# Second attention layer: one score unit as two halves of two heads, and its logarithm one place later

## The reference

```python
def _stablemax3_s(x):
    pos = 1.0 + x * (1.0 + 0.5 * x * (1.0 + x / 3.0))
    neg = 1.0 / (1.0 - x * (1.0 - 0.5 * x * (1.0 - x / 3.0)))
    return jnp.where(x >= 0, pos, neg)

def stablemax3(logits, axis=-1):
    logits = logits - jnp.max(logits, axis=axis, keepdims=True)
    s = _stablemax3_s(logits)
    return s / jnp.sum(s, axis=axis, keepdims=True)
...
attn = jnp.einsum('bhsd,bhtd->bhst', q, k) * scale
attn = stablemax3(attn, axis=-1)
out = jnp.einsum('bhst,bhtd->bhsd', attn, v)
```

## Time and profile before

| what | value |
|---|---|
| median of 3 runs | 5062.23 us (5046.65 to 5062.62) |
| the profiled execution | 5072.4 us, around a span of 5070.6 us |
| mean granted clock of PE over the span | 0.856 |
| PE, DVE, ACT, POOL busy | 3905.7, 2461.1, 1575.5, 323.2 us |
| from the first to the last square of the stage | 541.8 us |
| its busy time: PE, DVE, ACT | 404.8, 228.6, 449.5 us of 545.3 |

### The profile page before, as it was taken

The page is one execution under the profiler, slowest core; times in us unless marked ns, Lnnn a source line. Parts: engine busy times, 40 slices in busy tenths (PEclk is TensorE's granted clock), DMA queues, the critical chain, the costliest instruction groups (busy, mean ns, idle before and its releaser), DMA issues. The chain is left out here.

```text
span 5070.6 us, 97683 instructions
## 1 busy us (share of the span) xinstructions
PE 3905.7 (77%) x38224; PEld 2797.4 (55%) x38224; DVE 2461.1 (49%) x6959; ACT 1575.5 (31%) x2611; POOL 323.2 (6%) x451
## 2 busy tenths in 40 slices
PE   1259737988796999946887777568888888888899
PEld 1236524656465777733443333257667676676776
DVE  8636544532241000024554444277667676676762
ACT  0012202235202222211217888223322323323331
POOL 0011110000032000041000000000000000000000
PEclk8579868999757999977987787579999999999997
DMA  1281131011224454432000000200000000000000
GB/s 32 80 352 32 41 124 53 19 27 31 67 94 173 175 175 175 173 123 77 16 14 15 13 17 13 103 6 12 9 11 8 9 12 9 11 8 9 8 6 3
DMA packets 162722, 296.02 MB, mean 58 GB/s; under 512 B 36688, under 2 KB 138944, under 8 KB 154480
## 3 DMA queue, kind: packets, MB, share of 16 engines
q1 hardware_dynamic: 118336, 195.52, 12.5%
q10 hardware_dynamic: 37680, 77.59, 4.0%
q0 software_dynamic: 6272, 16.85, 1.0%
HBM read 184.17 MB, written 105.20 MB: 57 GB/s over the span
## 5 line engine op out<-in xcount | busy, mean ns | idle before, releaser
L2242 PE MATMUL peer_total<-peer_up,peer_hid 128*128 128x256 f32 (+1 forms) x2112 | 603.5, 410 | 2.2
L2172 PE MATMUL peer_work<-peer_xnT,peer_down 128*128 128x256 f32 (+1 forms) x2176 | 564.0, 388 | 41.0 <-issue 40.3
L2172 PEld LDWEIGHTS peer_work<-peer_xnT,peer_down 128*128 128x128 f32 x2176 | 428.6, 203 | 130.1 <-issue 50.5
L2269 ACT ACTIVATE peer_hid<-peer_work 128x256 f32<-128x256 f32 (+1 forms) x544 | 202.0, 371 | 833.5 <-PE peer_work L2172 833.5
L2230 PE MATMUL peer_scat<-peer_one_j,peer_one_i 64*64 64x32 f32 x16448 | 319.9, 228 | 136.7 <-DVE peer_one_j L2373 106.6
L2242 PEld LDWEIGHTS peer_total<-peer_up,peer_hid 128*128 128x128 f32 (+1 forms) x2112 | 379.7, 192 | 71.4 <-issue 10.8
L2230 PEld LDWEIGHTS peer_scat<-peer_one_j,peer_one_i 64*64 64x64 f32 x16448 | 293.0, 144 | 223.3 <-issue 223.2
L2291 ACT ACTIVATE peer_G<-peer_scat 128x512 f32<-128x512 f32 x258 | 273.0, 1058 | 360.0 <-PE peer_scat L2230 360.0
L2390 DVE TENSOR_TENSOR peer_hid<-peer_hid,peer_G 128x256 f32<-128x256 f32 (+1 forms) x544 | 215.6, 408 | 321.3 <-ACT peer_hid L2269 304.4
L1723 PE MATMUL moe_bank<-moe_xgT,moe_w 128*128 128x256 f32 x1280 | 294.9, 384 | 52.9 <-ACT moe_mid L1802 45.6
L1945 DVE TENSOR_TENSOR moe_yb<-moe_bank,moe_w 128x512 f32<-128x512 f32 x40 | 27.7, 692 | 624.5 <-PE moe_bank L1735 624.5
(11 more groups left out here) (361 smaller groups left out, 6250.5 us busy)
## 6 DMA issues: line engine op xcount, KB each, us to landing
moe_w<-in_moe_w SPq DMA_DIRECT2D x40, 2180.0 KB, 8.8
ys<-ret_zeros ACTq DMA_DIRECT2D x16, 2296.0 KB, 52.5
moe_xg<-xs SPq DMA_DIRECT2D x40, 256.0 KB, 8.8
ys<-moe_yb ACTq DMA_DIRECT2D x40, 256.0 KB, 9.1
soft_xT<-xT SPq DMA_DIRECT2D x32, 257.0 KB, 2.8
stable_xT<-xT SPq DMA_DIRECT2D x32, 257.0 KB, 2.8
ret_xT<-xT SPq DMA_DIRECT2D x16, 257.0 KB, 2.8
aT<-ret_cN SPq DMA_DIRECT2D x64, 64.2 KB, 2.1
```

The source lines that it names most:

```text
L2172: last = mm(work[:, jj % 2, 0:nb], down[:, c, jj, :], xnT[:, q, c, 0:nb], start=c == 0, stop=c == DC - 1)
L2242: last = mm(total[:b_rows, j, :], hid[:, e % NHID, j * P:j * P + b_rows], up[:, e, :], start=e == 0 and j == 0, stop=e == JB - 1, skip_gro ...
L2269: A(hid[:, jj % NHID, 0:nb], work[:, jj % 2, 0:nb], ACT.Gelu).then_inc(gelu_ready, 1)
```

## The change

A unit's four banks are treated as two halves of two banks (two heads). PE makes the scores of the first two heads as soon as DVE has freed their banks, tells ACT, waits for the other two banks and makes the other two. ACT squares each half by an instruction of its own, DVE multiplies and adds each half by an instruction of its own and frees the half's banks. The logarithm and the exponential still take a whole unit, but the logarithm of a unit now stands behind the first half-square of the next unit, and the exponential behind its second half-square. The first attention layer keeps its order.

```diff
@@ scores (PE)
-                else:
+                elif causal:
                     pe.wait_ge(s_taken, n)
...
                 stand()
+                if not causal:
+                    for x in range(2):
+                        if n:
+                            pe.wait_ge(s_taken, 2 * n + x - 1)
+                            stand()
+                        for j in range(2 * x, 2 * x + 2):
+                            rows = slice(SLOT * j, SLOT * j + SLOT)
+                            last = mm(S[:, j, 0:T], KT[rows, g, hg, k * P:k * P + P], QT[rows, g, hg, :], start=True, stop=True)
+                        last.then_inc(s_ready, 1)
+                    return
...
@@ weigh, log (ACT)
-                else:
-                    if n >= 2:
-                        act.wait_ge(ln_ready, n - 1)
-                    A(U[:, n % 2, :, :], S[:, :, 0:T], ACT.Square, scale=-SCALE, bias=bend[:, :]).then_inc(y_ready, 1)
-
-            def log(g, v):
-                n = g * SU + v
-                act.wait_ge(t_ready, n + 1)
...
+            def square(n, x):
+                act.wait_ge(s_ready, 2 * n + x + 1)
+                if n >= 2:
+                    act.wait_ge(ln_ready, n - 1)
+                A(U[:, n % 2, 2 * x:2 * x + 2, :], S[:, 2 * x:2 * x + 2, 0:T], ACT.Square, scale=-SCALE, bias=bend[:, :])\
+                    .then_inc(y_ready, 1)
+
+            def log(n):
+                act.wait_ge(t_ready, 2 * n + 2)
                 if n >= nw:
                     act.wait_ge(av_done, (n - nw) // 2 + 1)
                 A(W[:, n % nw, :, :], U[:, n % 2, :, :], ACT.Ln, scale=-1.0).then_inc(ln_ready, 1)
@@ the order on ACT
-                        weigh(g, v)
-                        if not causal and g + v:
-                            exponential(g * SU + v - 1)
-                        if not causal:
-                            log(g, v)
+                        if causal:
+                            weigh(g, v)
+                        else:
+                            n = g * SU + v
+                            square(n, 0)
+                            if n:
+                                log(n - 1)
+                            square(n, 1)
+                            if n:
+                                exponential(n - 1)
                     if not causal and g == B and s == 0:
+                        log(B * SU - 1)
                         exponential(B * SU - 1)
@@ cubic (DVE)
-                u = U[:, n % 2, :, :]
-                dve.wait_ge(y_ready, n + 1)
-                v_.scalar_tensor_tensor(u, u, REST, S[:, :, 0:T], ALU.add, ALU.mult).then_inc(t_ready, 1)
-                dve.wait_ge(t_ready, n + 1)
-                dve.sem_inc(s_taken, 1)
+                for x in range(2):
+                    u = U[:, n % 2, 2 * x:2 * x + 2, :]
+                    dve.wait_ge(y_ready, 2 * n + x + 1)
+                    v_.scalar_tensor_tensor(u, u, REST, S[:, 2 * x:2 * x + 2, 0:T], ALU.add, ALU.mult).then_inc(t_ready, 1)
+                    dve.wait_ge(t_ready, 2 * n + x + 1)
+                    dve.sem_inc(s_taken, 1)
```

More of the change, by code:

```diff
@@ L1050, in scores @@
                 stand()
+                if not causal:
[8 more added lines that the diff above has]
+                    return
                 for j in range(SLOTS):
                     rows = slice(SLOT * j, SLOT * j + SLOT)
-                    if causal:
-                        mm(S[:, j, 0:T], KT[rows, g, hg, 0:P], QT[rows, g, hg, :], start=True, stop=False, skip_group_check=True)
-                    else:
[L1056 to L1063, removed]
+                    mm(S[:, j, 0:T], KT[rows, g, hg, 0:P], QT[rows, g, hg, :], start=True, stop=False, skip_group_check=True)
+                for j in range(SLOTS):
+                    rows = slice(SLOT * j, SLOT * j + SLOT)
+                    mm(S[:, j, T:SPAN], KT[rows, g, hg, P:2 * P], QT[rows, g, hg, P:T], start=False, stop=False, skip_group_check=True)
+                for j in range(SLOTS):
+                    for at in (0, T):
+                        last = masked(S[:, j, :], at, 1)
                 last.then_inc(s_ready, 1)
@@ L1183, in weigh @@
                 act.wait_ge(s_ready, n + 1)
[L1184 to L1190, removed]
-                    if n >= 2:
-                        act.wait_ge(ln_ready, n - 1)
-                    A(U[:, n % 2, :, :], S[:, :, 0:T], ACT.Square, scale=-SCALE, bias=bend[:, :]).then_inc(y_ready, 1)
-            def log(g, v):
-                n = g * SU + v
-                act.wait_ge(t_ready, n + 1)
+                if n >= nw:
+                    act.wait_ge(av_done, n - nw + 1)
+                A(W[:, n % nw, :, :], S[:, :, 0:SPAN], ACT.Exp, scale=SCALE).then_inc(w_ready, 1)
+                act.wait_ge(w_ready, n + 1)
+                act.sem_inc(s_taken, 1)
+            def square(n, x):
[6 more added lines that the diff above has]
+                act.wait_ge(t_ready, 2 * n + 2)
                 if n >= nw:
```

## The result

The changed kernel takes 5100.5 us (median of 5 runs, 5095.7 to 5115.5) where the kernel before takes 5059.6 (5 runs): a ratio of 1.0093, 95% interval 1.0071 to 1.0115. It is slower by about 41 us, well clear of that interval.

What follows compares the result with a forecast made beforehand. The prediction took the ring and PE's clock to bound the stage. A batch falls from 34.1 to 31.6 us, times 16 a gain of 40, so the median goes from 5062.2 to 5022 us; range 4990 to 5060.

Steps and rivals of the forecast that it cites:

- second rival: In the stage, even units' scores queue behind earlier products at half clock: kernel slower, 5096 us at clock 0.77; chance 0.09.
- the same line: Forecast time of a batch after the change against PE's granted clock c: 30.0 + 27.0 (1 - c) us.
- ACT and DVE: ACT's unit 3.07 us, half-squares 0.67, logarithm's wait from 50 to under 10 us; DVE's half multiply-adds 0.73, covered.
- PE at full clock: A pair of scores keeps PE as long as four; lateness adds 0.9, so a batch takes 30.0 us against 31.5.
- PE at half clock: Doubled scores make PE the bound: a pair of units takes 8.8 us against 7.96, 3.4 more a batch.
- The clock: PE's usual granted clock in the stage taken as 0.91, with PE held 82% at full clock; a batch 31.6 us.
- become shorter: Argument against the no-change rival (chance 0.13): PE's idle stretches, 2.01 us before scores, shrink.
- packing: Four heads' scores run side by side on PE; splitting into pairs adds 83 us of PE time; no-change chance 0.13.
- a clock at or below 0.85 with ACT waiting for scores after products: Sign of being wrong: low granted clock in the stage while ACT waits for scores queued behind PE's products.
- DVE's copies delaying the first multiply-add: Sign of being wrong: on DVE, copies hold up a unit's first half multiply-add; no size given.
- break-even clock: Granted clock of 0.85 in the stage, under which the forecast batch exceeds the 34.1 us of before.
- the ring: In a unit before the change: square, multiply-add, logarithm, then ACT free for the next square, 3.36 us.

Runs made afterwards that it cites:

- e4: The changed kernel plus five discarded matmuls a batch where PE stood idle, behind the spreads of units 4 and 6: 5017.2 us, 0.9920 of before.
- e13: The changed kernel plus five discarded matmuls a batch behind the products of unit 7, where PE leaves no gap: 5142.7 us, 1.0171 of before.
- e7: The changed kernel plus three discarded matmuls a batch, behind the spread of unit 6 only: 5059.4 us, 1.0001 of before.
- e1: The kernel before with only the logarithm moved behind the next unit's square, nothing halved: 5019.2 us, 0.9918 of before.
- e2: The changed kernel with ACT's old order: half-squares side by side, exponential of the unit before, then this unit's logarithm: 5054.1 us, 0.9996 of before.
- e3: Halves on ACT and DVE in the old order, but PE's four heads of scores made side by side: 5016.2 us, 0.9918 of before.
- e14: Whole scores, halves on ACT and DVE, logarithm behind both half-squares, first value unit two steps later, no added matmuls: 5038.1 us, 0.9956 of before.
- e10: The changed kernel with the first value unit at step 3 instead of 1: 5099.4 us, 1.0073 of before.

## Why the prediction was wrong

The forecast was 5022 us, a gain of 40; the kernel lost 41. The mechanism was in the main the one that the prediction had as its second rival, "PE becomes the bound at half clock", at a chance of 0.09: ACT waits 57.0 us for scores queued behind other work of PE. What the rival did not name is the odd score at half clock, 47.5 us of ACT's waits. That its 5096 us lies near the measured 5100 is luck: it belongs to a clock of 0.77, and at the measured 0.68 the same line gives 38.6 us a batch, 72 us more than before.

**ACT and DVE** were right: the half-square took 0.68 for 0.67, and the logarithm's wait was 0.0 for "under 10". By the Trainium skill ("ScalarE: Activation LUTs", What ACT_TABLE_LOAD costs) a square of 514 columns would last 280 + 0.833 x 514 = 708 ns, an estimate from its figures; the trace has 680.

**PE at full clock** was right. A half keeps PE as long as the four heads (0.70 and 0.72). In e4 the odd score comes 0.4 late where 0.5 was forecast, and a batch at clock 0.95 takes 31.2 us, where 30.0 + 27.0 x 0.05 gives 31.4.

**PE at half clock** was priced a little too high, which does not explain a loss. The last batch, all at 0.50, gives 28.7 us for seven units, 8.2 a pair, where 8.8 was forecast and 7.96 measured before. Late halves do run side by side in part: the scores at 2970.25 are eight records within 0.72. At a clock of 0.68 the measured batch is 37.5, for the line's 38.6.

**The clock** was the step that failed: "I take 0.91, the best of now, as the usual clock." It was 0.67. The prediction reached for 0.91 because PE would be held 82% of the time at full clock, and without gaps at half clock. It had written that "the busy share alone does not tell the clock", and then took it as the argument. Its argument that PE's idle stretches "become shorter" held in the sum: PE idled 139.0 us ahead of scores before the change and 88.3 after it. The clock fell even so. What the prediction left out is where the gaps lie. PE's scores used to be one block of eight records behind one wait. Now ACT's logarithm stands between the two half-squares, so the two halves wait 1.5 us apart, and behind units 4 and 6, where little else is queued, PE idles 1.0 to 1.6 us, makes one half in 0.7, idles 0.8 and makes the other. The clock falls at just those places. The work that is then due, products and odd score of unit 5, comes at 1.2 GHz and makes ACT wait; ACT's delay opens the next gap.

That the clock is the cause is shown by intervention: e4 works on two of the gaps, adds work to PE and takes 67.5 us off the stage; e13 adds the same work elsewhere and puts 52.6 on it; e7 works on one gap and takes off 24.7. That the gaps come from split and order together is read from e1, e2 and the traces: the order alone (e1) is faster than before, the split in the old order (e2) is no slower, and only both together lose. That packing acts mainly through the clock is likely but not shown: making the scores whole (e2 to e3) raised it from 0.74 to 0.83 and took 17 us from first to last unit, while e14, with whole scores too but at 0.76, takes 529.1 us, hardly less than e2's 534.4 with scores in pairs. But e14 also has the logarithm moved and the first value later.

What stays open is why some gaps bring the clock down and others don't. In the kernel before, PE idled 2.01 us ahead of scores in a stretch that stayed at 1.00; in e2 the 1.02 ahead of unit 5's scores brought no fall; in the changed kernel, 1.01 and 0.82 with a short piece of work between them came ahead of one. Nor is it shown that idle time alone counts: the added matmuls use all 128 rows of PE, the scores of a half 64, and no run filled the gaps with work as narrow as theirs.

Of the signs of being wrong that the prediction listed, "a clock at or below 0.85 with ACT waiting for scores after products" came true. "DVE's copies delaying the first multiply-add" occurs too (45.8 us of waits), but nearly as much before the change (40.5), and e10 took most of it away without a gain.

## What to carry to other kernels

Before a block of PE work is cut into parts that wait for each other, look at where PE will idle between the parts, not only at whether its sum still fits: the granted clock is a term of the sum, and where a sum hangs on it, its break-even clock belongs next to a reason for the clock itself. Splitting the elementwise engines' instructions cost nothing (e3). Splitting the four-head scores opened the harmful gaps only where ACT's order also pulled the two halves apart (the change against e2), so two edits that are harmless one by one are to be tried together before they are trusted. And before a chain is split at all, try moving one instruction out of the ring: e1 gave the same 0.8% by moving the logarithm alone.

## What the runs showed of the hardware that was not expected

Five matmuls a batch whose result nobody reads made the changed kernel 83 us faster where PE stood idle, and 42 us slower where it did not. In the kernel before they were worth 24 us in the medians, but only 6.6 from first to last unit.

Batches 1 to 14 of the changed kernel repeated one pattern, each 37.5 us long, with PE busy 31.8 us of it at a clock of 0.68 in the one shown. The last batch, with PE busy 25.45 of 28.7 us, stayed at 0.50 throughout.
